# Attention and expert layers on eight cores: the f32 projection weights are cast once into bf16 copies in device memory, and the projection passes load the copies through SyncE's queue

## What is computed

```
x = x + attention(layernorm(x))        # its own layernorm again inside, 16 heads of 64
    q = xn @ Wq ; k, v = split(xn @ Wkv)          # Wq 1024x1024, Wkv 1024x2048, float32
    q = rotary(q) / 8 ; k = rotary(k) ; k = k @ W_bilinear[head]
    out = softmax(q k^T) v ; out @ Wo
x = x + experts(layernorm(x))          # 8 experts, top 2 by a gate, hidden 2048, relu
```

## Time and profile before

| | us |
|---|---|
| median of 3 runs | 5043.61 |
| lowest and highest of them | 4898.96, 5107.69 |
| the profiled execution, its own time | 4899.81 |
| its span, slowest core (core 1) | 4898.3 |
| block `s0`, up to the first instruction of `attnA` on SyncE | 23.2 |
| projection pass 0 | 23 to about 587 |
| projection pass 1 | 1475 to about 1885 |
| output projection, gate and experts | from about 2797 |

### The profile page before, as it was taken

The page is one execution under the profiler, slowest core; times in us unless marked ns, Lnnn a source line. Parts: engine busy times, 40 slices in busy tenths (PEclk is TensorE's granted clock), DMA queues, the critical chain, the costliest instruction groups (busy, mean ns, idle before and its releaser), DMA issues. The chain is left out here.

```text
span 4898.3 us, 41832 instructions; the slowest of 8 cores (4886.4 to 4898.3 us)
## 1 busy us (share of the span) xinstructions
PE 3585.0 (73%) x15474; PEld 1327.9 (27%) x15474; DVE 971.4 (20%) x1750; ACT 1628.7 (33%) x1747; POOL 41.6 (1%) x66
## 2 busy tenths in 40 slices
PE   4444547777774345777777651999999999999999
PEld 1111101111111111111111121344444444444444
DVE  2333341111113333111111344101000111000111
ACT  1111017777771110777777111111222111222111
POOL 0000000000000000000000000000000000000000
PEclk9666758888886666888888575999999999999999
DMA  3434200000004220000000150011213030303031
GB/s 73 69 52 60 35 0 1 1 1 1 1 1 86 61 52 17 1 1 1 1 1 1 32 123 1 1 34 36 48 22 69 1 69 1 69 1 69 15 81 43
DMA packets 34665, 150.00 MB, mean 31 GB/s; under 512 B 2828, under 2 KB 2957, under 8 KB 32294
## 3 DMA queue, kind: packets, MB, share of 16 engines
q0 software_dynamic: 23952, 111.51, 13.6%
q1 hardware_dynamic: 10518, 35.83, 2.2%
HBM read 250.39 MB, written 8.39 MB: 53 GB/s over the span
## 5 line engine op out<-in xcount | busy, mean ns | idle before, releaser
L667 ACT ACTIVATE arena<-PB,arena 128x1024 bf16<-128x1024 f32 x1024 | 1101.0, 1112 | 427.1 <-PE PB L658 419.0
L687 PE MATMUL PB<-arena 128*128 128x512 bf16 x2048 | 701.9, 428 | 301.0 <-ACT arena L667 271.4
L1032 PE MATMUL PB<-arena 128*128 128x512 bf16 x4096 | 895.7, 380 | 31.0 <-ACT arena L1013 28.8
L1006 PE MATMUL PB<-arena 128*128 128x512 bf16 x4096 | 892.1, 380 | 0.0
L1013 ACT ACTIVATE arena<-PB,arena 128x512 bf16<-128x512 f32 x512 | 351.9, 687 | 1445.8 <-PE PB L1006 1445.8
L1032 PEld LDWEIGHTS PB<-arena 128*128 128x128 bf16 x4096 | 396.5, 98 | 522.8 <-issue 54.5
L1006 PEld LDWEIGHTS PB<-arena 128*128 128x128 bf16 x4096 | 401.0, 98 | 485.2 <-issue 4.5
L1048 DVE SCALAR_TENSOR_TENSOR arena<-PB,arena 128x512 f32<-128x512 f32 x256 | 192.3, 751 | 1630.5 <-PE PB L1032 1412.3
L658 PE MATMUL PB<-arena 64*128 64x512 bf16 x2048 | 441.8, 439 | 0.0
L687 PEld LDWEIGHTS PB<-arena 128*128 128x128 bf16 x2048 | 137.9, 100 | 644.9 <-issue 643.5
L703 DVE COPY arena<-PB 1x512 f32<-1x512 f32 x64 | 44.1, 689 | 1341.6 <-PE PB L687 1341.6
(11 more groups left out here) (131 smaller groups left out, 1345.6 us busy)
## 6 DMA issues: line engine op xcount, KB each, us to landing
arena<-wkv POOLq DMA_DIRECT2D x32, 1024.0 KB, 9.9
arena<-w1t POOLq DMA_DIRECT2D x8, 4096.0 KB, 26.2
arena<-w2t POOLq DMA_DIRECT2D x8, 4096.0 KB, 26.3
arena<-x_roll SPq DMA_DIRECT2D x48, 512.0 KB, 3.3
arena<-wq POOLq DMA_DIRECT2D x8, 1024.0 KB, 10.0
out<-arena SPq DMA_DIRECT2D x16, 512.0 KB, 2.6
arena<-wo POOLq DMA_DIRECT2D x1, 2048.0 KB, 20.0
arena<-costab SPq DMA_DIRECT2D x2, 512.0 KB, 4.9
```

The lines of the kernel that those rows point to most:

```text
L667: l_exp = P.op("scalar", (lambda par, pr: lambda e: e.activation(out=a_pt2[par], in_=PB[:, par * 1024:(par + 1) * 1024], func=AF.Exp, bias ...
L687: e.matmul(pb[ob][0:128, :], a_v[:, js * VTW + h * (DH + 1): js * VTW + h * (DH + 1) + 128], pt, start=(js == 0), stop=(js == 15)))(
L1006: e.matmul(pb[b], f_w1[:, d * HID + hf * 128: d * HID + (hf + 1) * 128], f_ln2T[:, d * OWN + tc * 512: d * OWN + (tc + 1) * 512], start=(d ...
L1032: last = e.matmul(pb[b], f_hT[:, hf * 512 + m4 * 128: hf * 512 + (m4 + 1) * 128], f_w2[:, hf * D + oh * 512: hf * D + (oh + 1) * 512], sta ...
```

## The change

Three tensors in device memory are added: `kpre`, `vpre` and `qpre`, each two halves of 128 partitions by 4096 bf16, in the order in which the staging buffers want them. At the end of GpSimd's part of `s0`, six transfers on its queue, each waited for before the next, cast the six halves of the k, v and q weights from float32 into these tensors; they go from device memory to device memory. `predone` names the last one's landing. `wload` then loads a half from its copy, already bf16 and 8 KB contiguous in each partition, on SyncE's queue instead of GpSimd's, and waits for `predone` as well. Numbers and results are rounded as before, only once instead of at each load.

```
+    kpre = dt("kpre", [2, 128, 4096], BF16).ap()      # and vpre, qpre
 ...
+        pre_done = None
+        for half in range(2):
+            for nm, dstp, col0, wsrc in (("k", kpre, 0, wkv), ("v", vpre, D, wkv),
+                                         ("q", qpre, 0, wq)):
+                pre_done = P.dma("pre", "gsdma", (lambda dstp, half, col0, wsrc: lambda e:
+                    e.dma_start(
+                        out=dstp[half].rearrange("p (c f) -> p c f", f=D),
+                        in_=wsrc[half * 512:(half + 1) * 512, col0:col0 + D]
+                        .rearrange("(c p) f -> p c f", p=128)))(dstp, half, col0, wsrc),
+                    serialize=True)
+        P.labels["predone"] = P.labels[pre_done]
         P.op("vector", lambda e: e.memset(s_mx[0:1, :], -1e30), signal="mxinit")
 ...
                 def wload(which, half):
                     sbuf = a_wstg[half]
-                    (src: 512 rows of wkv or wq, "(c p) f -> p c f")
-                    l_w = P.dma(f"ws{half}", "gsdma", dma(dst, src),
-                                waits=[wstg_free[half]])
+                    srcp = {"k": kpre, "v": vpre, "q": qpre}[which][half]
+                    l_w = P.dma(f"ws{half}", "sync", dma(sbuf[:, 0:4 * D], srcp),
+                                waits=[wstg_free[half], "predone"])
                     return sbuf, l_w
```

More of the change, by code:

```diff
@@ L181, in build_nc @@
     identf = dt("identf", [128, 128], F32, kind="ExternalInput").ap()
+    kpre = dt("kpre", [2, 128, 4096], BF16).ap()
+    vpre = dt("vpre", [2, 128, 4096], BF16).ap()
+    qpre = dt("qpre", [2, 128, 4096], BF16).ap()
     out = dt("out", [OWN, D], F32, kind="ExternalOutput").ap()
```

## The result

| | us |
|---|---|
| before, median of 10 runs | 4897.17 |
| changed kernel, median of 10 runs (lowest, highest) | 5054.94 (4944.25, 5229.98) |
| ratio, changed to before | 1.0104, 95% interval 1.009 to 1.0118 |

The ratio puts the changed kernel at about 4948 us. In some executions of either kernel (28 of the kernel before's 53 in the later series, 9 of the changed kernel's 15 in all) the chip grants some cores a lower TensorE clock in part of the program, which adds 30 to 400 us; six of the ten runs of the changed kernel in the table were such, and the ratio leaves them out.

The account below looks back on a forecast made before the run. No transfers as a whole bound the kernel, TensorE being busy 3585.0 of 4898.3 us; 4899.8 + 64.8 (copies in s0) - 10.0 (pass heads) + 0 (loads on SyncE) = 4954.6, say 4955 us, range 4925 to 5033.

Parts of the forecast that it names:

- the last one of the sum: Whole kernel: read the change against the profiled 4899.8 us, lowest run, with the median 2.9% and the highest 4.2% above.
- No transfer bounds the kernel, no weight load is waited for: Projection sweeps: all 40 weight loads are hidden; only VectorE's first x tile of each pass is waited for, 26.9 us.
- The block's exit passes the copies on in full: End of s0: all engines wait for GpSimd's six copies, so attnA starts at 88.0 instead of 23.2, +64.8 us.
- The price of a link: Copies in s0: each takes 11.1 us plus 0.6 for the turn to the next issue, six links 70.2 us.
- The quarter of the way towards 14.8: Copies in s0: 11.1 us each, between the wkv load's 9.9 and 14.8 if device memory's bytes set the pace.
- The pass heads: Start of both passes: the first x tile lands sooner without k halves beside it, 3.3 + 6.7, -10.0 us.
- The landing of 7.3 us: Start of each pass: the first x tile lands 7.3 us after issue instead of 10.6 in pass 0, 14.0 in pass 1.
- Order on SyncE: Forty loads moved to SyncE: 0 us; as a rival, costly from 14 us a load, 5019 at 18, chance 0.03.
- Slow copies: Copies in s0 at 23.1 us each give 5027 us; decides from 18.3; chance 0.16, of which 0.12 beyond 18.3.
- Quick copies: Copies in s0 at the w1t load's rate, 6.6 us each, 43 us in all, kernel at 4928; chance 0.08.
- Hidden: Other engines don't wait for GpSimd at s0's end; first sweep waits on predone, 4899.8 + 9 - 10; chance 0.04.
- A real gain: Whole kernel: 98 us out of stages where nothing waits for a weight; chance 0.01.

Follow-up runs that it names:

- the transfers into SBUF: The changed kernel with its six serialized casting transfers in s0 writing into the staging buffers in SBUF instead of device memory; 4950.24 us in the profiled execution.
- the loads alone: The kernel before, without copies, its passes loading bf16 halves on SyncE's queue from a constant in device memory; ratio 0.9997 to the kernel before.
- the experiment with the copies beside the pass: The changed kernel with the six copies issued at the start of the first projection pass, each staging load waiting for its own half; ratio 1.0001 to the kernel before.

## Why the prediction was right or wrong

**The range was wrong.** The median of ten runs, 5054.9, lies outside 4925 to 5033. The step that failed is the last one of the sum: it saw that two of three runs of the kernel before stood 2.9% and 4.2% above the third, found no row that explained it, and then put that term at nothing, as if the changed kernel's runs would all be like the lowest. What the runs showed in its place: a lower granted clock lengthened six of the ten, by 81 to 282 us over the 4948 of the ratio, which puts the median 107 us above it. In the first profile of the changed kernel the time lies in the expert stage, at a clock of 0.86 instead of 0.95 and 201 us longer on the slowest core. The change is not shown to bring this about: such executions were 2 of the ten of the kernel before (median 4897.17) against 6 of the changed kernel's ten, but 28 of 53 against 9 of 15 over the later series and all of the changed kernel's runs. What lowers the clock stays open. A range for a median of runs has to take in what the runs at hand show; a forecast of the change alone, 4955, belonged beside it, in words. Against the 4948 that the ratio gives, the forecast of the change was 7 us off.

**No transfer bounds the kernel, no weight load is waited for**: right, to a tenth of a us in each of TensorE's waits at the heads of the sweeps.

**The block's exit passes the copies on in full**: right. 57.1 us later, twelve copies another 58.7, and nothing once they leave the block.

**The price of a link**: 11.7 us taken, 10.4 measured (80.3 less 0.3 for the exit and 17.9 for the first issue, over six). The nearest row, 9.9 and 0.6, alone would have given 10.5. The quarter of the way towards 14.8, added for the writes into device memory, was not needed; set against the transfers into SBUF the writes cost about 0.5 us a link. With this term mis-sized, the start of attnA came 7.7 us before its forecast (80.3 against 88.0). That a link is landing plus turn gave nearly the right sum, but it isn't why the chain is that long: without any turn, six take about 61 us instead of 62.

**The pass heads**: -10.0 taken, -8.8 measured as the shortening of the two blocks (4.1 and 4.7). The size is right partly by luck. The landing of 7.3 us was worked out well: 7.0 and 6.4 were measured, medians of the cores. But the 14.0 from which it was taken in pass 1 is core 1's, the longest of the eight (9.5 to 14.0, median 10.3), so that 3.0 and not 6.7 was to be had there on a middle core. And the loads alone gave 1.1 and 2.9; the rest came only with the copies, for a reason that stays open.

**Order on SyncE**: cost nothing, as said. With both k halves and an x tile in the queue a k half lands after 7.3 us in the median, far under the 14 at which it would have begun to count.

**The rivals.** Slow copies: no, 9.8 us in the median against the 18.3 that decide. Quick copies: no. Hidden: no, and the experiment with the copies beside the pass shows how they would have had to be placed for that. (Its sum also left out the staging load behind the last copy, 6.6 us by its own bound, so nearer +6 than no change.) A real gain: none of 2%, with or without the copies' cost.

## What to carry to other kernels

Before making a transfer cheaper, look for an engine that waits for it: forty loads land in 5 to 7 us here instead of 10, and no wait at the head of a sweep changed by more than a tenth of a us. Preparation that is waited for in front of a block's exit is paid by all engines, but for what the block had left (57 of 62 us here); the same preparation, each consumer waiting for its own part, was free. At the head of a stage put what the first computation needs ahead of what is needed later: that was worth 12 to 15 us, where the prepared weights were worth 2 us at the most. And where runs at hand stand apart without a row that explains it, a range for their median has to reach over all of them.

## What the runs showed that was not expected

- Six casting copies within device memory take as long in flight together (about 61 us) as one after the other (about 62 us), and as long with 3120 packets as with 6000. A single one lands in about 10 us, so a longer queue buys next to nothing at this size when all cores copy, though it raises the busy share of the transfer engines from 0.70 to 0.99.
- Serial chains of large transfers pull the cores apart: entries into attnA lie within 1.2 us before, 8.2 us apart behind six copies in turn (10.0 behind twelve), with one core of a pair 4.5 to 5.2 us behind the other. With the six in flight together they lie within 2.8 us.
